# The output copies of a local attention, half of them moved from ACT to DVE

## The reference

```python
Bx, Tx, C = x.shape                     # 4, 1024, 64; x is the layer-normed h
q = x @ wq.T                            # 16 heads of 64
kv = x @ wkv.T                          # one key head, one value head
q = _rmsnorm(_rope(q), q_norm_w)
k = _rmsnorm(_rope(k), k_norm_w)
mask = (cols <= rows) & (rows - cols <= 128)
scores = jnp.einsum('bqgtd,bqgsd->bqgts', q, k) * scale
scores = jnp.where(mask[None, None, None], scores, NEG)
attn = jax.nn.softmax(scores, axis=-1)
out = jnp.einsum('bqgts,bqgsd->bqgtd', attn, v)
return out @ wo.T
```

## Time and profile before

| | us |
|---|---|
| median of three runs | 1003.0 |
| the profiled execution | 998.69 |
| its span | 996.9 |
| PE busy in the span | 755.8 |
| DVE busy | 637.8 |
| ACT busy | 448.5 |
| POOL busy | 382.7 |
| ACT's exps, L743, 512 of them | 242.9 |
| ACT's output copies, L731, 128 of them, 378 ns each | 48.4 |
| DVE's pT copies, L702, 128 of them, 824 ns each | 105.5 |
| DVE's row maxima, L691, 128 of them, 833 ns each | 106.6 |

### The profile page before, as it was taken

The page is one execution under the profiler, slowest core; times in us unless marked ns, Lnnn a source line. Parts: engine busy times, 40 slices in busy tenths (PEclk is TensorE's granted clock), DMA queues, the critical chain, the costliest instruction groups (busy, mean ns, idle before and its releaser), DMA issues. The chain is left out here.

```text
span 996.9 us, 21354 instructions
## 1 busy us (share of the span) xinstructions
PE 755.8 (76%) x8244; PEld 484.7 (49%) x8244; DVE 637.8 (64%) x1277; ACT 448.5 (45%) x1398; POOL 382.7 (38%) x432
## 2 busy tenths in 40 slices
PE   5578799777999587996869999996899964501870
PEld 5232677333775325773327764673577741301550
DVE  0477688485886666884768885677477747600780
ACT  0012899124995227991229972421666630200200
POOL 0035466154663353661436651471100000074475
PEclk9989999899999899998899999997999996755965
DMA  8144000080000440000710000005100021014300
GB/s 289 47 170 81 2 3 2 3 240 11 3 2 2 171 82 2 2 2 3 226 24 2 2 2 1 1 3 87 21 2 2 2 76 42 1 48 92 58 20 13
DMA packets 60142, 45.89 MB, mean 46 GB/s; under 512 B 51761, under 2 KB 57357, under 8 KB 59125
## 3 DMA queue, kind: packets, MB, share of 16 engines
q1 hardware_dynamic: 57590, 37.22, 14.6%
q10 hardware_dynamic: 144, 4.19, 1.1%
q0 software_dynamic: 2304, 3.04, 0.9%
HBM read 29.64 MB, written 7.15 MB: 37 GB/s over the span
## 5 line engine op out<-in xcount | busy, mean ns | idle before, releaser
L743 ACT ACTIVATE work<-ps,small,rq 128x160 f32<-128x160 f32 x512 | 242.9, 486 | 14.9 <-DVE small L694 14.8
L722 POOL TENSOR_TENSOR work<-work,small 128x512 f32<-128x512 f32 x128 | 133.1, 1040 | 148.5 <-DVE small L708 148.5
L691 DVE TENSOR_REDUCE ps<-ps 128x4 f32<-128x640 f32 x128 | 106.6, 833 | 59.2 <-PE ps L631 58.8
L265 PE MATMUL ps<-xT,s_proj_w 64*128 64x512 f32 x288 | 83.9, 704 | 47.5 <-DVE prod L573 26.7
L702 DVE COPY pT<-ps 128x640 f32<-128x640 f32 x128 | 105.5, 824 | 7.9 <-PE ps L644 7.9
L743 ACT ACTIVATION_READ_ACCUMULATOR work<-ps,small,rq 128x1 f32 x512 | 104.6, 204 | 0.0
L631 PE MATMUL ps<-kT,big 64*128 64x160 f32 x1024 | 100.9, 318 | 0.0
L1413 POOL DMA_INDIRECT sent_rows<-big,xb x32 | 30.9, 965 | 180.1 <-DVEq L1365 170.7
L601 POOL TENSOR_TENSOR big<-prod 128x1024 f32<-128x1024 f32 x32 | 75.3, 2359 | 50.5 <-DVE prod L573 50.3
L661 PE MATMUL ps<-pT,vwin 128*64 128x128 f32 x1024 | 84.2, 282 | 10.2 <-ACT big L731 2.4
L631 PEld LDWEIGHTS ps<-kT,big 64*128 64x128 f32 x1024 | 78.8, 197 | 0.1
(11 more groups left out here) (265 smaller groups left out, 1362.6 us busy)
## 6 DMA issues: line engine op xcount, KB each, us to landing
xb<-in_x SPq DMA_DIRECT2D x4, 4096.0 KB, 12.3
xb<-in_x ACTq DMA_DIRECT2D x1, 4096.0 KB, 15.1
vrem<-hl SPq DMA_DIRECT2D x64, 64.0 KB, 2.1
sent_rows<-empty_row SPq DMA_DIRECT2D x8, 325.0 KB, 9.4
s_proj_w<-in_proj_w SPq DMA_DIRECT2D x1, 1536.0 KB, 6.3
big<-sent_rows SPq DMA_DIRECT2D x5, 264.0 KB, 5.2
big<-sent_rows SPq DMA_DIRECT2D x5, 256.0 KB, 4.6
xb<-in_ffn_w SPq DMA_DIRECT2D x1, 1028.0 KB, 4.8
```

The costliest lines, as they stand in the source:

```text
L265: ins = nc.tensor.matmul(bank[banks + w][:], proj_w[half_rows(w), cols], xT[half_rows(w), :], start=True, stop=True)
L691: ch.step(v.tensor_reduce(row_max(c), ps[:, s_banks(c), 0:2 * SPAN].rearrange("p e (h k) -> p e h k", h=2), X, ALU.max))
L722: g.tensor_tensor(probs[:, c % 3, :, 0:P], probs[:, c % 3, :, 0:P], bc(small[:, c % 4, 3, :], P), ALU.mult)
L743: nc.scalar.activation(probs[:, c % 3, q, :], bank[2 * (c % 2) + e][:, SPAN * hh:SPAN * hh + SPAN], ACT.Exp, bias=small[:, c % 4, 1, q:q + ...
```

## The change

The output of an even chunk is copied by ACT as before, at the same place in ACT's program. The output of an odd chunk is copied by DVE, in its step c + 5, between the bias of that step and the copy into pT. DVE's copies count in a semaphore of their own, oT_dve. values(c) waits for the copy of chunk c - 1 as before: for odd c that is ACT's, for even c DVE's. DVE's loop gets two more steps for the last copies.

```diff
                 def values(c):
                     pe.wait_ge(S["pT_ready"], c + 1)
                     if c >= 1:
-                        pe.wait_ge(S["oT_ready"], c)
+                        pe.wait_ge(S["oT_ready" if c % 2 else "oT_dve"], (c + 1) // 2)
...
-                pe.wait_ge(S["oT_ready"], CHUNKS)
+                pe.wait_ge(S["oT_ready"], CHUNKS // 2)
+                pe.wait_ge(S["oT_dve"], CHUNKS // 2)
...
-                for n in range(CHUNKS + 3):
+                def outputs(c):
+                    v.wait_ge(S["pv_done"], c + 1)
+                    v.tensor_copy(oT[:, :, CHUNK * c:CHUNK * (c + 1)].rearrange("p (h a) t -> p h a t", h=2),
+                                  ps[:, 6:8, 0:P].rearrange("p h (a t) -> p h a t", t=CHUNK)).then_inc(S["oT_dve"], 1)
+
+                for n in range(CHUNKS + 5):
...
+                    c = n - 5
+                    if c >= 0 and c % 2:
+                        outputs(c)
                     c = n - 3
-                    if c >= 0:
+                    if 0 <= c < CHUNKS:
...
                     for q in range(NQ):
-                        if q == 2 and c >= 4:
+                        if q == 2 and c >= 4 and c % 2 == 0:
                             outputs(c - 4)
...
-                for c in range(CHUNKS - 4, CHUNKS):
+                for c in range(CHUNKS - 4, CHUNKS, 2):
                     outputs(c)
```

More of the change, by code:

```diff
@@ L199, in program @@
             "v_dve", "kprod", "scores_done", "bias_ready", "exp_done", "scaled", "transposed",
-            "pT_ready", "pTr_ready", "pv_done", "oT_ready", "wo_done", "sums_inverted",
+            "pT_ready", "pTr_ready", "pv_done", "oT_ready", "oT_dve", "wo_done", "sums_inverted",
             "zero_done", "slots_ready", "pool_chain", "sent", *(f"back{k}" for k in range(CHUNKS_X)), "turned_back", "hid_act",
```

## The result

The kernel with the change takes 1056.53 us in the median of four runs (1052.75 to 1067.88); the kernel before, 1005.91 in four. The ratio is 1.054, 95% interval 1.043 to 1.066: slower. The profiled execution took 1055.03 us, 56.3 more than the 998.69 of before; the medians lie 50.6 apart.

A forecast was written before the change was run, and what follows sets the result against it. No engine has much room, so the order of one pair of steps (4.37 us) decides. 998.69 us plus 54.6 (52 pairs x 1.05) plus 1 for stage ends gave 1054, stated as 1055 us; range 1038 to 1076.

The forecast's parts named there:

- The wait that moves: Values of even chunks wait for DVE's copy behind maximum and bias: start 2.40 us after scores, not 1.26; step 3.37.
- The copy: DVE's new output copy, between bias and pT copy: taken as 0.43 us, from a copy of 256 f32 PSUM elements.
- The bound of 0.82: Upper bound for DVE's new copy: the pT copy of 640 PSUM elements, 0.82 us each, giving 1075 us.
- The odd step: PE's odd step, both copies already done: at most 2.14 us, not below 1.66, taken as 2.05.
- Rival 1: PE catches up in the odd step, running it at 1.66 us: +0.66 us a pair, 1034 us; chance 0.06.
- The covers: Delayed pT copy, ACT's copy (waits about 0.6 us) and layer norm (0.8 us before PE wants it) stay hidden.
- ACT's saving at nothing: One ACT copy of 0.27 us a pair is gone; costed at nothing, as exps wait for bias, scores and PE.
- The sum: Four stages: 52 pairs x 1.05 us = 54.6, plus 1 for stage ends, on 998.69: 1054, stated as 1055 us.
- Rival 2, the clock: PE's clock falls in the new gaps of the steps: +2.8 us a pair, about 1200 us; chance 0.03.

The follow-up runs named there:

- e1_head: Changed kernel with DVE's odd output copy at the head of its step, ahead of the maximum: 1010.25 us, ratio 1.002 to the kernel before.
- e3_all_dve: Changed kernel with all 32 output copies of a stage on DVE, each behind the bias: 1131.73 us, ratio 1.123 to the kernel before.
- e10_no_copies: Changed kernel with no output copies on any engine and without PE's waits for them: 997.05 us, ratio 0.983 to the kernel before.
- e4_odd_left_out: Changed kernel without DVE's copies of odd outputs and PE's waits for them: 1009.89 us, ratio 1.003 to the kernel before.
- e11_copy_twice: Changed kernel with DVE's output copy made twice, first into a place nobody reads: 1090.98 us, ratio 1.079 to the kernel before.
- e5_late: Changed kernel with DVE's output copy behind the copy into pT instead of ahead of it: 1171.15 us, ratio 1.161 to the kernel before.
- e7_all_head: Changed kernel with all 32 output copies of a stage on DVE, at the head of its step: 1005.11 us, ratio 0.999 to the kernel before.
- e8_end_of_step: Changed kernel with DVE's odd output copy one step earlier, behind the reciprocal: 1007.75 us, ratio 0.993 to the kernel before.
- e12_end_again: The kernel of e8_end_of_step run again with more rounds: 1011.91 us, ratio 1.005 to the kernel before.

## Why the prediction was right

The time was forecast at 1055 us and is 1056.53; every step can be held against a row.

- **The wait that moves.** Forecast 2.40 us from the scores to the values of an even chunk, measured 2.39 (157.02 to 159.41). The even step was put at 3.37 and is 3.36. e1_head shows that the place in DVE's program does it, e3_all_dve that it does so in whatever step it stands.
- **The copy.** Put at 0.43 us by the copy of the same size, measured 0.414. The bound of 0.82 was far off.
- **The odd step.** Put at 2.05 us, measured 2.03. Rival 1 had PE catch up to 1.66 on the ground of its weight loads; it falls. The step with neither of the two waits is 2.03 in the changed kernel, in e1_head (152.65 to 154.68) and in e10_no_copies (150.88 to 152.91). So 2.03 us is PE's own pace at full clock, 4.06 a pair, 93% of the pair of 4.37. In the window of the earlier trace rows matmuls kept PE busy for 97% and weight loads for 76%: here the matmuls' share told PE's room better. The Trainium skill, "Perfetto Trace Analysis", section "Identifying the Most-Contended Engine", would take the weight loads' share; these runs don't bear that out.
- **The covers.** ACT's wait ahead of its copy was put at 0.6 and is 0.51 us; it stayed covered, and so did the copy into pT (its end, 159.99, lies before the transposes of the odd step). The layer norm stayed hidden, with 1.04 us to spare where 0.8 was forecast.
- **ACT's saving at nothing.** e4_odd_left_out gives nothing, as costed. The reason given, that the exps start from the bias, was right for the even chunks, whose own chain of 4.37 us contains the copy that stayed.
- **The sum.** 52 x 1.05 + 1 = 55.6 was forecast. The rows give 52 x 1.02 = 53 and 2 more in one stage with a slow start, and 56.3 in the profiled execution. The 0.03 us by which the pair was too long, 1.6 us in all, paid for a clock that I hadn't in the sum. Outside the stages single stretches moved by more than the 1.0 us that they leave in the sum: from the first stage's last maximum to the second's first it is 75.2 us instead of 69.0, at a clock of 0.86 instead of 0.95, and later stretches took most of it back. So the agreement to 1.5 us is partly luck; runs of one kernel spread over 15 us, and the medians differ by 50.6 where 55.6 was forecast.
- **Rival 2, the clock.** It did not come in the changed kernel, and it was the one mechanism that my expectations for the experiments left too small: in the runs with pauses of 1.43 and some 1.9 us it came.

## What to carry to other kernels

Before a piece of work is moved to another engine, ask what stands ahead of it in that engine's program, and whether any of that waits for the engine that waits for the piece. A copy of 0.4 us in the wrong place cost 1.0 us a pair of steps; the same copy 1.5 us earlier in the step (0.31 behind the scores instead of 1.83) cost nothing. An engine that is busy all the time need not be the bound: look for the chain of one period through all engines, and for the next one right below it, before you count a saving.

## What the runs showed of the hardware

**Repeated pauses of PE went with a lower clock in two runs, and not in two others.** With pauses of 1.09 us in a pair of 5.39 the clock was 1.00 once the start of a stage was over. With 1.43 in 5.72 it fell once in each stage and was 0.95 to 0.98 inside the stages. With 1.84 to 2.0 in 6.13 it fell in about every second pair and was 0.83 to 0.88. The share of idle time does not order the runs: e3_all_dve pauses for 1.25 us in every step of 3.35, has PE busy for a smaller part of its time than any of the others, and stays at 1.00:

```profile
460.00:545.00 85.00, 53.80 (x928) 42.28 (x922) 54.40 (x128) 51.35 (x208) 36.21 (x52) 1.00 0.01 2
```

What decides is not shown; among these four runs the clock fell in the two whose single pauses were the longest. The Trainium skill describes a clock that swings when PE pauses often and briefly in "TensorE: Matmul & The Clock Gate", section "A second HAM failure mode: psum-queue depth-cycling". The traces of e11_copy_twice and e5_late agree; those of the changed kernel and of e3_all_dve, with pauses as frequent or more so, do not.

The clock made the price of a wait steeper than one for one. From e11_copy_twice to e5_late a pair at full clock grows by 0.41 us (5.72 to 6.13), 21 us in 52 pairs; the stages grow by 58 us in sum (348.6 to 406.4), and the whole time by 80 (1171.15 - 1090.98).

**The first ten microseconds of a stage.** They are the same work in every stage, but the clock that they get differs. Windows of 10 us from the first scores, one for the kernel before, two for the changed one, one for e7_all_head:

```profile
239.00:249.00 10.00, 6.45 (x74) 5.41 (x76) 5.60 (x13) 7.33 (x31) 3.46 (x5) 0.83 0.00 1
```

```profile
257.10:267.10 10.00, 7.11 (x60) 5.98 (x58) 5.05 (x12) 7.22 (x31) 3.44 (x5) 0.50 0.00 1
411.60:421.60 10.00, 6.45 (x74) 5.42 (x76) 5.50 (x13) 7.32 (x31) 3.45 (x5) 0.83 0.00 1
```

```profile
249.00:259.00 10.00, 7.11 (x61) 5.97 (x60) 5.05 (x12) 7.27 (x31) 3.50 (x5) 0.50 0.00 1
```

At 0.50 a stage is 2 us longer than at 0.83: 82.9 against 80.9 us in the changed kernel (whose first stage, at 0.71, took 80.9 too). All four stages of the kernel before started at 0.83, all four of e7_all_head at 0.50, and that is where its gain of 2 us a stage went in that execution. Whether its program makes that start or chance does, one trace can't say. Two traces of one kernel say that the program alone does not always decide it: in e8_end_of_step the third stage is the long one (69.4 us, the others 67.3 to 67.5), in e12_end_again the first (69.5, the others 67.4).
